# Cross-attention scores from stacked float32r parts that go by way of DRAM, with seven stages and another order on every engine

## The reference

```python
# layer 0: cross attention, 16 heads of 8 features
q, k, v = x @ Wq + bq, ctx @ Wk + bk, ctx @ Wv + bv          # split into 16 heads of 8
scores = q k^T / sqrt(8); scores = .5 * (scores * mask) + .5 * scores; clip to +-50; softmax
x = layer_norm(x + context @ Wo + bo) * gamma + beta
# layer 1: causal attention in segments of 64, 16 heads of 64, rotary
mem = rms_norm(mean(ctx)) @ to_mem_tokens                     # one token, counted 16 times
q, k, v = rms_norm(x) @ to_qkv_w;  q, k = rope(q), rope(k)
keys = [memory token, 16 persistent keys, the segment's keys]
x = x + softmax(q k^T / 8) v @ to_out_w
x = x + (silu(g) * a) @ ff_w2 + ff_b2,  [a, g] = rms_norm(x) @ ff_w1 + ff_b1
```

## Time and profile before

| | |
|---|---|
| median of 3 runs | 1216.44 us (1213.78 to 1217.11) |
| the profiled execution: time, span | 1214.23 us, 1212.4 us |
| busy: PE, weight loads | 1163.1 us (96%), 1019.5 us (84%) |
| busy: DVE, ACT, POOL | 987.0 us (81%), 1009.3 us (83%), 993.7 us (82%) |
| DMA engines, mean share | 27.7% |
| granted TensorE clock | 0.996 of full speed |

### The profile page before, as it was taken

One profiled execution on the slowest core, in us unless ns is written; L12 is line 12 of the kernel. 1 busy time (PEld: TensorE's weight loads), 2 busy tenths in 40 slices (PEclk: granted clock), 3 DMA queues, 4 the chain that ended last, 5 costly groups with the idle time before them and its releaser, 6 DMA issues.

```text
span 1212.4 us, 54784 instructions
## 1 busy us (share of the span) xinstructions
PE 1163.1 (96%) x20707; PEld 1019.5 (84%) x20707; DVE 987.0 (81%) x2574; ACT 1009.3 (83%) x3341; POOL 993.7 (82%) x1678
## 2 busy tenths in 40 slices
PE   3799999999999999999999999999999999999985
PEld 2588888888888888888888888888888888888874
DVE  5578888888888888888888888888888888888872
ACT  1488888888888888888888888888888888888874
POOL 1578988888888888888888888888888888888874
PEclk9999999999999999999999999999999999999999
DMA  8122222222232223222222222322222222222220
GB/s 222 59 99 90 84 98 87 82 98 100 69 102 100 80 87 102 86 83 98 87 82 98 91 78 100 102 71 96 102 82 87 98 87 82 98 87 82 99 82 28
DMA packets 54344, 110.43 MB, mean 91 GB/s; under 512 B 9557, under 2 KB 28586, under 8 KB 54186
## 3 DMA queue, kind: packets, MB, share of 16 engines
q1 hardware_dynamic: 54314, 110.01, 27.7%
HBM read 21.63 MB, written 4.46 MB: 22 GB/s over the span
## 4 chain that ended last, share of the span: by engine, by line
PE 91%; DVE 3%; ACT 2%; DMA 1%; issue 1%; POOL 1%; SPq 0%; POOLq 0%; ACTq 0%; DVEq 0%
PE psum L968 18%; PE psum L1042 9%; PE psum L990 7%; PE psum L1023 7%; PE psum L975 6%; PE psum L1010 6%; PE psum L981 5%; PE psum L998 5%; PE psum L1111 4%; PE psum L961 3%; PE psum L1016 3%; PE psum L963 2%; PE psum L1127 2%; PE psum L962 2%; PE psum L999 2%; PE psum L1145 2%
## 5 line engine op out<-in xcount | busy, mean ns | idle before, releaser
L626 ACT ACTIVATE probs<-psum,less_max 128x81 f32<-128x81 f32 x1024 | 236.9, 343 | 50.8 <-DVE less_max L810 50.8
L968 PE MATMUL psum<-xnT,wqkv 128*128 128x128 f32 x2048 | 252.3, 277 | 0.9 <-ACT xnT L583 0.5
L968 PEld LDWEIGHTS psum<-xnT,wqkv 128*128 128x128 f32 x2048 | 240.3, 193 | 1.5 <-DVE z L806 0.7
L505 POOL TENSOR_TENSOR probs_near<-probs,rden 128x256 f32<-128x256 f32 x256 | 157.3, 614 | 71.9 <-DVE rden L894 71.9
L796 DVE TENSOR_TENSOR ra<-psum,rope 128x512 f32<-128x512 f32 x256 | 174.7, 682 | 12.9 <-PE psum L968 5.9
L497 POOL TENSOR_TENSOR kall<-ra,rs 128x512 f32<-128x512 f32 x128 | 162.8, 1272 | 21.2 <-DMA rs<-rb 9.7
L796 DVE TENSOR_TENSOR rb<-psum,rope 128x512 f32<-128x512 f32 x256 | 174.0, 680 | 0.0
L806 DVE TENSOR_TENSOR z<-psum,wT 77x512 f32<-77x512 f32 x256 | 163.7, 679 | 8.4 <-PE psum L975 2.5
L495 POOL TENSOR_TENSOR qT<-ra,rs 128x512 f32<-128x512 f32 x128 | 162.9, 1273 | 0.0
L501 POOL TENSOR_SCALAR z<-z 77x512 f32<-77x512 f32 x256 | 151.6, 609 | 7.9 <-DVE z L806 7.9
L652 ACT ACTIVATE z<-z 77x512 f32<-77x512 f32 x256 | 141.4, 648 | 8.7 <-POOL z L501 8.7
(11 more groups left out here) (135 smaller groups left out, 2887.7 us busy)
## 6 DMA issues: line engine op xcount, KB each, us to landing
rs<-rb SPq DMA_DIRECT2D x256, 256.0 KB, 2.3
vals_far<-vals SPq DMA_DIRECT2D x128, 128.0 KB, 2.3
seq_in<-in SPq DMA_DIRECT2D x64, 230.5 KB, 2.6
out<-out_sb SPq DMA_DIRECT2D x64, 64.0 KB, 1.6
ctx_all<-in SPq DMA_DIRECT2D x5, 320.0 KB, 9.4
wqkv<-in SPq DMA_DIRECT2D x1, 1536.0 KB, 14.0
vals_pre<-memv_dram SPq DMA_DIRECT2D x64, 4.0 KB
ctx_all<-in SPq DMA_DIRECT2D x3, 288.0 KB, 7.1
```

The costliest lines, as they stand in the source:

```text
L505: nc.gpsimd.tensor_tensor(probs_near[:, slots, :], probs[:, slots, 0:SEG], scale.broadcast_to([S, 4, SEG]), ALU.mult)
L626: last = nc.scalar.activation(probs[:, 4 * t + n, :], at(f"scores{t}")[:, KEYS * n:KEYS * (n + 1)], ACT.Exp, bias=less_max[:, 4 * t + n:4 ...
L968: last = mm(at(name)[:, S * n:S * (n + 1)], wqkv[:, lo + 128 * n:lo + 128 * (n + 1)], xnT[:], start=n == 0)
```

## The change

The cross scores are made in another way. After the q/k/v product of layer 0 each of q and k is split in two float32r parts, a rounded one and the rest. `qk_parts` holds three parts of each (q: rounded, rest, rounded; k: rounded, rounded, rest), so that the sum of the three products is the score. SP stores it in DRAM (`qk_dram`) and loads it back into `qk_stack` by four DMAs, so that a head's eight features of the three parts lie on 24 consecutive rows. A cross score is then one float32r product over 24 rows; there are 16, as before, on the same four row groups, each of 77 by 128. The weights wq and wk have their columns interleaved on the host for this. `kz`, `qb` and `own_rows` go. The making of the parts and the copy of v0 are three instructions on ACT and two on DVE (before, three on DVE).

There is one stage more (LEAD 7): qkv is at k = 7 (its load) and 6, cross at 6 (product) and 5, c0T, wo and the layer norm at 5, scores 0 and 1 and v1, v0 at 4. Every engine has another order, and the banks are dealt anew. The swap DMAs go by pair 0 and pair 1: swapped0 after q0_rotated, swapped1 after k1_rotated. `first_weights` and the second half of the context now follow the first sequence's stacks, and `other_weights` those of the second.

New order in a turn (number in brackets: k):

- PE: xnT(4), lin(1), k0, q0, k1(4), u(5), q1(4), turned0, turned1(3), hnT(2), turned2(3), pv(5), turned3(3), down(1), o0-o3(3), c0T(5), gate(2), wo(5), scores0(4), out(3), v1, v0(4), cross(6), qkv(7), scores1(4).
- ACT: values0(3), xn(4), k parts(6), x1sq(2), xnT(4), exp_cross 0, 3(5), exp_self 2(3), exp_cross 1, 2(5), exp_self 3(3), q parts, v0(6), u(5), mask1(4), hn(2), turned0, turned1(3), hnT(2), turned2(3), xnT_hi(4), turned3(3), wT(6), mask0(4), heads 2(3), c0T(5), heads 1, 0, 3(3), gated(2), exp_self 1, 0(4), values1(4), mask2(4), ysq(5), mask3(4).
- DVE: masked 3, 1(5), largest 3, reciprocal 1, largest 2(3), masked 2(5), reciprocal 0(3), rotate k0, q0(4), sums and reciprocals 2, 3(3) with the two rests of the parts(6) between, through_gate(1), rotate q1, k1(4), reciprocal of pv(5), out_sb(1), c0, r, bn, mean, variance(5), largest 1, 0(4), centred(5), x1(3), sum 1(4), y(5), sum 0(4), masked 0(6).
- POOL: clamp 0, 3, 1(5), power(2), raise(1), clamp 2(5), ug(1), normalised 1, 0, 2, 3(3), memory key, xnT_lo, sum q0, k0(4), x1b(2), xb(6), sum q1(4), power(5), y_keep, sum k1(4), power(5).

The diff, cut to its core (the bodies of the engines are the lists above; shown of them are new instructions, new waits and SP whole):

```diff
-MEANS, POOLED, TOKENS_A, TOKENS_B = 7, 7, 6, 3
-LEAD = 6
+MEANS, POOLED, TOKENS_A, TOKENS_B = 1, 1, 0, 3
+LEAD = 7
...
+        qk_dram = nc.dram_tensor("qk_dram", (3, D, S + S2), F32, kind="Internal").ap()
...
-        qb = sb("qb", [D, S])
-        kz = sb("kz", [D, GROUP, S2])
+        qk_parts = sb("qk_parts", [D, 3, S + S2 + 1], F32R)
+        qk_stack = sb("qk_stack", [128, GROUP, S + S2 + 1], F32R)
...
+            ("q0", 0, 4, (q0_rotated,)),
+            ("turned1", 0, 3, (probsT1_ready,)),
+            ("turned3", 0, 3, (probsT3_ready,)),
+            ("o3", 0, 3, (oT3_ready,)),
+            ("xs1", 0, 6, (z1_masked,)),
...
                 if seq[3] is not None:
-                    sp.wait_ge(k0_rotated, done[4])
+                    sp.wait_ge(vals0_ready, done[4])
                     passed(sp, sp_passed)
-                    for odd in range(2):
-                        sp.dma_start(rs[odd::2, half(0)], rb[1 - odd::2, half(0)]).then_inc(swapped0_in, 16)
...
+                    sp.dma_start(vals_far[0:SEG, :, :].rearrange("k c e -> k (c e)"), vals[SEG:2 * SEG, 0:BANK]).then_inc(vals_far0_in, 16)
                 if seq[0] is not None:
                     sp.wait_ge(out_ready, done[1])
                     passed(sp, sp_passed)
                     sp.dma_start(out[bass.ds(seq[0], 1), :, :].rearrange("b s d -> (b s) d"), out_sb[:]).then_inc(out_stored, 16)
                 if seq[3] is not None:
...
+                    if first(seq[3]):
+                        store_memory_values()
+                    sp.dma_start(vals_pre[0::BAND, :, :].rearrange("n (f h) d -> n f (h d)", f=2),
+                                 memv_dram[bass.ds(seq[3], 1), :].rearrange("b (f n e) -> (b n) f e", f=2, n=4)).then_inc(memv_in, 16)
+                if seq[4] is not None:
+                    sp.wait_ge(q0_rotated, done[5])
                     passed(sp, sp_passed)
...
+                    for odd in range(2):
+                        sp.dma_start(rs[odd::2, half(0)], rb[1 - odd::2, half(0)]).then_inc(swapped0_in, 16)
+                if seq[6] is not None:
+                    sp.wait_ge(k_rest_ready, done[7])
                     passed(sp, sp_passed)
...
+                    sp.dma_start(qk_dram.rearrange("t p s -> p t s"), qk_parts[:, :, 0:S + S2].bitcast(F32)).then_inc(parts_out, 16)
+                if seq[4] is not None:
+                    sp.wait_ge(k1_rotated, done[5])
                     passed(sp, sp_passed)
                     for odd in range(2):
                         sp.dma_start(rs[odd::2, half(1)], rb[1 - odd::2, half(1)]).then_inc(swapped1_in, 16)
                 if seq[6] is not None:
-                    if first(seq[5]):
+                    sp.wait_ge(parts_out, done[7] * 16)
+                    passed(sp, sp_passed)
+                    for r in range(GROUP):
+                        sp.dma_start(qk_stack[32 * r:32 * r + 3 * HD0, :, 0:S + S2].bitcast(F32),
+                                     qk_dram.rearrange("t (d r g) s -> r (t d) g s", r=GROUP, g=GROUP)[r]).then_inc(stacks_in, 16)
+                    if first(seq[6]):
                         context_loads(2, 3)
                         first_weights()
...
+                    if first(seq[5]):
+                        other_weights()
+                if seq[7] is not None:
+                    wait(sp, wT_ready, done[7])
+                    wait(sp, xb_ready, done[7])
                     passed(sp, sp_passed)
...
+                    sp.dma_start(seq_in[:], seq_pack[bass.ds(seq[7], 1), :, :].rearrange("b p n -> (b p) n")).then_inc(inputs_in, 16)
+                    if first(seq[7]):
                         context_loads(0, 1)
+                if seq[4] is not None:
+                    sp.wait_ge(vals1_ready, done[5])
+                    passed(sp, sp_passed)
+                    sp.dma_start(vals_far[SEG:2 * SEG, :, :].rearrange("k c e -> k (c e)"), vals[0:SEG, BANK:2 * BANK]).then_inc(vals_far1_in, 16)
...
+                    pool.wait_ge(inputs_in, done[7] * 16)
+                    wait(pool, r_ready, done[6])
+                    nc.gpsimd.tensor_tensor(xb[:], x_sb[:], bo_rep[:], ALU.add).then_inc(xb_ready, 1)
...
+                if seq[6] is not None:
+                    act.wait_ge(qkv_filled, done[7])
+                    nc.scalar.activation(qk_parts[:, 0:2, S:S + S2], at("qkv")[:, S:S + S2].unsqueeze(1).broadcast_to([128, 2, S2]), ACT.Identity,
+                                         bias=cols[:, BK:BK + 1])
...
+                if seq[6] is not None:
+                    nc.scalar.activation(qk_parts[:, 0::2, 0:S], at("qkv")[:, 0:S].unsqueeze(1).broadcast_to([128, 2, S]), ACT.Identity,
+                                         bias=cols[:, BQ:BQ + 1])
+                    wait(act, u_filled, done[6])
+                    copy(v0[:, :, 0:HD0], at("qkv")[0:S2, 256:384].rearrange("k (h d) -> k h d", h=H)).then_inc(v0_kept, 1)
...
-                    dve.wait_ge(qkv_filled, done[6])
-                    keys_of_heads()
-                    V.tensor_scalar(qb[:], at("qkv")[:, 0:S], cols[:, BQ:BQ + 1], None, ALU.add).then_inc(qb_ready, 1)
-                    V.tensor_copy(v0[:, :, 0:HD0], at("qkv")[0:S2, 256:384].rearrange("k (h d) -> k h d", h=H)).then_inc(v0_kept, 1)
...
+                if seq[6] is not None:
+                    dve.wait_ge(v0_kept, done[7])
+                    V.scalar_tensor_tensor(out=qk_parts[:, 1, 0:S], in0=at("qkv")[:, 0:S], scalar=cols[:, BQ:BQ + 1],
+                                           in1=qk_parts[:, 0, 0:S].bitcast(F32), op0=ALU.add, op1=ALU.subtract)
+                    if first(seq[6]):
+                        sum_tokens(0)
+                        sum_tokens(1)
+                    V.scalar_tensor_tensor(out=qk_parts[:, 2, S:S + S2], in0=at("qkv")[:, S:S + S2], scalar=cols[:, BK:BK + 1],
+                                           in1=qk_parts[:, 0, S:S + S2].bitcast(F32), op0=ALU.add, op1=ALU.subtract).then_inc(k_rest_ready, 1)
...
+                if seq[5] is not None:
+                    if first(seq[5]):
+                        context_totals()
                     dve.wait_ge(rden0_ready, done[6])
...
             def cross_scores():
-                for n in range(GROUP):
+                for g in range(GROUP):
                     for r in range(GROUP):
-                        rows = slice(32 * r, 32 * (r + 1))
-                        last = mm(at(f"xs{r}")[0:S2, S * n:S * (n + 1)], kz[rows, n, :], qb[rows, :])
+                        part = slice(32 * r, 32 * r + 3 * HD0)
+                        last = mm(at(f"xs{r}")[0:S2, S * g:S * (g + 1)], qk_stack[part, g, S:S + S2], qk_stack[part, g, 0:S])
                 return last
...
+                    pe.wait_ge(stacks_in, done[7] * 64)
+                    cross_scores().then_inc(xs_filled, 1)
```

More of the change, by code:

```diff
@@ L325, in build @@
[L325 to L333, removed]
+            ("xnT", 3, 4, (xnT_ready,)),
+            ("lin", 5, 1, (sT_ready,)),
+            ("k0", 4, 4, (k0_rotated,)),
@@ new lines, in build @@
+            ("scores0", 1, 4, (probs0_exp,)),
+            ("o0", 7, 3, (oT0_ready,)),
+            ("o1", 2, 3, (oT1_ready,)),
+            ("o2", 6, 3, (oT2_ready,)),
+            ("o3", 0, 3, (oT3_ready,)),
+            ("c0T", 3, 5, (c0T_ready,)),
+            ("gate", 5, 2, (gate_ready,)),
+            ("wo", 6, 5, (y_ready,)),
+            ("out", 7, 3, (x1_ready,)),
+            ("v1", 2, 4, (vals1_ready,)),
+            ("v0", 3, 4, (vals0_ready,)),
+            ("xs0", 4, 6, (z0_masked,)),
@@ L980, in weigh_cross @@
                     head = GROUP * g + r
[L981 removed]
+                    last = mm(at("u")[32 * r:32 * (r + 1), S * g:S * (g + 1)], v0[:, head, :], z0[:, head, :], start=g == 0)
                 return last
@@ L1129, in body @@
                 if seq[3] is not None:
+                    free(pe, "turned3", n)
+                    pe.wait_ge(probs3_ready, done[4])
+                    turn(3).then_inc(turned3_filled, 1)
+                if seq[1] is not None:
+                    free(pe, "down", n)
+                    pe.wait_ge(sT_ready, done[2])
+                    for i in range(FCH):
+                        last = mm(at("down")[:, 0:D], sT[0:FROWS[i], i, :], w2[0:FROWS[i], i, :], start=i == 0, stop=i == FCH - 1)
+                    last.then_inc(down_filled, 1)
+                if seq[3] is not None:
                     if first(seq[3]):
@@ new lines, in body @@
+                if seq[3] is not None:
+                    free(pe, "out", n)
+                    pe.wait_ge(oT3_ready, done[4])
+                    for i in range(PAIRS):
+                        last = mm(at("out")[:, 0:D], oT[:, i, :], wout[:, i, :], start=i == 0, stop=i == PAIRS - 1)
+                    last.then_inc(out_filled, 1)
+                if seq[4] is not None:
+                    if first(seq[4]):
+                        pe.wait_ge(wv_lo_ready, 1)
+                    free(pe, "v1", n)
```

(3 more changed lines are left out.)

587 lines of the change are left out of this document (262 added, 325 removed).

## The result

| | before | after |
|---|---|---|
| median (lowest to highest) of 4 runs each | 1216.78 us (1213.78 to 1221.19) | 1258.13 us (1257.16 to 1262.50) |
| span of the profiled execution | 1212.4 us | 1255.8 us |

The ratio is 1.0344, with a 95% interval of 1.0304 to 1.0384. The forecast of 1210 us had the wrong sign, and the range of 1190 to 1246 didn't hold the time.

The account below looks back on a forecast made before the run. The prediction took PE, busy 17.85 us of a 17.93 us turn, to bound the kernel. Fill 82 + 60 turns x 17.5 + drain 76 = 1208 us, with 1.8 around it 1210; range 1190 to 1246.

Parts of the forecast that it names:

- Cross scores on PE: PE's cross-score slot falls from 1.05 to 0.45 us with 16 float32r records, saving 0.60 us per turn.
- rival 1: On PE, float32r with 128 columns is no faster: slot stays 1.05 us, turn 18.1, time 1246; chance 0.25.
- What bounds the kernel now: In the steady turn PE binds, busy 17.85 of 17.93 us; a microsecond less is worth some 60 us.
- second leg: From wo to the next k0, PE and the chain through layer norm and ACT both take 7.3 us: no stall.
- PE's turn: PE's work alone in a steady turn: 17.93 - 1.05 + 0.45 = 17.33, say 17.3 us.
- Does the new order keep PE fed: In the steady turn, o starts at 7.6 instead of 7.4, a 0.2 us stall, so the turn is 17.5 us.
- ACT: ACT's added copies of k parts, q parts and v0 take 0.8 us, making it 16.45 of 17.3 us.
- The way by DRAM: Parts' store and stack loads land at 14.1 us, wanted at 14.7: hidden behind PE's work, 0.6 us to spare.
- rival 2: Stacks come late from DRAM by 1.1 us more: PE stalls 0.5 us per turn, time 1240; chance 0.13.
- Fill and drain: At both ends: fourth sequence's qkv at 82 us (72 to 88), last qkv to the end 76 (70 to 82).
- The sum: Whole span: 82 + 60 x 17.5 + 76 = 1208 us; with 1.8 us around it, a time of 1210.

Follow-up runs that it names:

- Experiment 4: The kernel before, in its own order and six stages, with kz and qb in float32r, low parts left out, 16 cross-score records: 1215.4 us against 1215.5, ratio 0.9994.
- experiment 3: The changed kernel with its cross scores in float32 from the same stacks, 32 records instead of 16: 1294.8 us, ratio 1.0637 to the kernel before.
- experiment 5: The changed kernel with the third product (the xnT_lo term) of each value projection left out: 1254.1 us, ratio 1.0321 to the kernel before.
- Experiment 1: The changed kernel with the three DMA waits in front of o moved ahead of the waits for PSUM banks: 1250.3 us, ratio 1.0268 to the kernel before.
- experiment 2: The changed kernel with ACT's mask copy for scores1 moved behind its copy of turned3: 1258.7 us, ratio 1.0346 to the kernel before.
- experiment 7: The changed kernel with second context half and first weights issued behind the first inputs, and sequence 0's rests before its token sums: 1252.7 us, ratio 1.0306.
- experiment 11: The changed kernel with the reordered waits of Experiment 1 and the fill of experiment 7 together: 1239.9 us, ratio 1.0200 to the kernel before.
- experiment 8: The changed kernel with the DRAM store and stack loads done for the first sequence only, later ones reusing its stacks: 1253.0 us, ratio 1.0299.
- experiment 6: The changed kernel with waits before o reordered, two dropped, and ACT's c0T copy moved before the first copy of the heads: 1253.4 us, ratio 1.0309.

## Why the prediction was wrong

**Cross scores on PE: right.** 0.43 us for 0.45, and rival 1 with it was wrong.

**What bounds the kernel now: the step that failed in kind.** "A microsecond less of PE in a turn is worth some 60 us, but only down to where ACT, DVE and POOL or a chain through them bind, and these have 2.3 to 2.7 us to spare." The 2.3 to 2.7 us are idle time of engines, and no measure for a chain. Experiment 4 took 0.6 us from PE in the old order and found a chain 0.02 us below, over DVE, POOL and ACT. The earlier trace rows show PE busy for 17.85 of 17.93 us, and the earlier trace rows a chain that ended last with 91% PE; neither can tell a second chain that is as long. The busy time of PE also hid that it waited already: the 0.16 us in front of the cross scores mostly lie within the length of v0's last record. What the 60 us per microsecond are worth was therefore unproven for the old order, and in the new one I had found them both at 7.3 in the second leg, which experiments 3 and 5 confirm.

**PE's turn: mis-sized by 0.3 us.** I took the old turn, less the old slot, plus the new one: 17.33. Without the gap at `o` it is 17.6. The changes of tiling aren't the reason: "five before (u, o, two scores, cross), five after" holds, and they cost about 0.9 us in either kernel. The Trainium skill (TensorEngine Tiling (Array Packing), Key Properties) says that a change of tiling mode drains TensorE; the records agree and give the size, about 0.09 us in front of it and 0.05 to 0.10 behind. What the sum put at nothing are short waits. The old order had 0.16 us of them in front of the cross scores, which went; the new one has 0.43 us, and 17.33 - 0.16 + 0.43 is 17.6. At three of these places, in the turn shown, a result comes just too late: ACT's copy of xnT is done at 614.04 and k0 starts at 614.17, POOL's last division at 620.50 and turned3 at 620.64, ACT's copy of c0T at 624.68 and wo at 624.81. In front of xnT and lin PE's sequencer has register arithmetic of its own to do.

**Does the new order keep PE fed: right about the place, half of the cause missing, too small.** The stall at `o` was predicted at 0.2 us behind ACT's copy of turned3. The copy came on time, and 0.3 us of idle (0.4 by starts) followed. Experiment 1 showed that half of it is PE's sequencer working through waits that had long been met; the 0.2 us that are left there are the stall that was forecast. Before, the same waits stood in front of `o` too, but `gate` and `pv` lay between turned0 and `o`, 1.2 us of products, and the sequencer was done before PE was. In the new order only `down`, 0.67 us, lies between turned3 and `o`. The mask in ACT's queue had nothing to do with it (experiment 2). The second leg took 7.40 for 7.3.

**ACT: right.** 16.28 for 16.45. By busy time k parts have 0.45 us, q parts 0.49 and v0 0.27, more than the 0.8 us of slots together, but consecutive instructions overlap.

**The way by DRAM: right.** No PE wait for `qk_stack` in a steady turn (14.6 us in three waits, 13.9 of it the first), and rival 2 was wrong. The unevenness that it brings, 0.07 us per turn, I had not counted.

**Fill and drain: the fill right, the drain too short.** The fourth qkv came at 84.3 (predicted 82, bounds 72 and 88), the second at 35.4 (38). From the last qkv to the end it took 85.5 us instead of 76. I had added to the old 65.8 only what qkv's new place in its turn is worth. But a sequence now needs 5.5 turns from its qkv to `down` instead of 4.8 (99.2 us for 85.8, both for the 57th sequence), and the first turn without qkv is 19.0 us, longer than a full one:

```profile
1171.90:1190.90 19.00, 17.04 (x302) 14.94 (x303) 14.41 (x40) 16.43 (x57) 15.53 (x28) 1.00 0.34 108
```

PE is busy for less, and waits 1.4 us in front of scores1 for a mask; in POOL's timeline the swap that usually has landed is late (1.85 us of waiting):

```profile
1186.47 1.29 POOL L505 TENSOR_TENSOR qT<-ra,rs 128x512 f32<-128x512 f32 x1 [1.85 <-DMA rs<-rb]
```

**The sum.** 84.3 + 60 x 18.1 + 85.5 = 1255.8. Of the 48 us between this and the 1208 of the prediction 2 are the fill, 36 the turn, 10 the drain. Against the kernel before the shares are others: 60 turns at 0.1 to 0.16 us are 6 to 9 of the 43, the rest is the longer way at both ends.

**What stays open.** The seventh stage was not tried without the new order, so how the 36 us are split between the stage, the order and the two dependent transfers is read from the traces and not shown, except for the 5 us of experiment 7. Nor is it shown what makes the swap late in the first turn of the drain, why the same loop runs at 17.92 and at 17.80 us in experiments 1 and 11, and by what path the trip makes the turns uneven (the largest excesses stand in front of wo and near the end of `o`).

## What to carry to other kernels

An engine that is busy for 99% of a turn need not be the only bound: before counting a saving by the number of turns, follow the longest chain through the other engines around the turn as well, or take the saving away in one quick run (experiment 4 would have told at once that 0.6 us of PE were worth nothing in the old order). When products are put in a new order, ask of each pair that goes PE, ACT, PE what lies between, how many waits the sequencer has to go through behind the late one, and put that one last. And a longer way from the inputs to the result is paid at both ends. Here, with one more stage and a new order, it cost some 36 us; with 60 turns that is as much as 0.6 us in each of them.

## What the runs showed of the hardware

- A wait on PE's sequencer that is met still takes about 0.10 us when the sequencer isn't ahead: four instructions at 621.73, 621.84, 621.93 and 622.04. Where it is ahead of the products, such steps cost nothing: in the kernel before they stand in front of `o` at 605.27, 605.38, 605.48 and 605.58, and `o` follows at 605.74, 0.20 us behind the last record of pv, as at any change of tiling.
- float32r with 24 rows and 128 columns on four row groups takes 27 ns per record, float32 with 32 rows 33 ns at twice the records; 0.43 against 1.04 us for the same 16 products.
- In 3 of the 32 turns of the changed kernel that I averaged, PE stalls between the last records of `o` for 0.15 to 0.28 us, in one of them twice, at records that wait for nothing. In the kernel before and in experiment 8, which have no trip in their steady turns, no turn has that, but neither has one in experiments 6 and 7, which do have it. So it is not shown that the stalls follow from the trip's traffic.
